# Layer 1's ring loads moved ahead of the couples' loads, and layer 4's gate and up products placed on either side of an older unit's down product

## The chip, the cores and the metric

The kernel runs on one core of one Trainium2 chip. The metric is the device time of one execution in microseconds (us).

## The reference, cut to what matters

Four conditional layers run one after the other on `x` (16 samples of 128 tokens by 128 features, float32), each added to its input. `cond_8` (16 x 8) chooses.

```python
# layer 1 (L0_cond in the reference): one expert of 8 for each sample
hidden = silu(x @ wu[e].T + bu) * (x @ wg[e].T + bg)   # 128 -> 256
x = x + hidden @ wd[e].T + bd                          # 256 -> 128
x = x + x @ W_base.T + b_base + lora(x, cond_8)        # layer 2
x = x + x @ w_bot(cond_8).T + bias                     # layer 3
# layer 4 (L3_cond): the two best of 8 experts for each sample, and a shared one
out = sum over the two e: w_e * (gelu(x @ gate_e) * (x @ up_e)) @ down_e    # 128 -> 512 -> 128
x = x + out + (gelu(x @ shared_gate) * (x @ shared_up)) @ shared_down
```

## The kernel before, in words

**Layer 1.** The 16 samples are taken in turn. Each needs its expert's pack (386.5 KB), which SyncE (SP) loads into `ring0`, a ring of 8 slots (`SLOTS0`); `load0(b)` (L255 to L260) does it. It reads sample b's expert number out of SBUF with a register load of its own (L256), waits from b = 8 on until sample b - 8 has been finished (`x1_done`), and issues the DMA (L259). TensorE runs `upgate0(b + 1)` ahead of `down0(b)` (L467, L475), ScalarE the SiLU (L392), VectorE the gate's multiply (L690) and the sum into `x` (L704).

**SP's order.** SP is one queue in program order: `load0` for samples 0 to 7, the shared expert's pack (768 KB), a wait for the sort of layer 4 (`slots_done`) and a register load of 24 expert numbers (L241), then `load_duo(0)` (L265), `load0(8)`, `load0(9)`, `load_duo(1)`, `load0(10)` to `load0(15)`, and the packs of the solos (L274). A couple's or a solo's pack has 768 KB. Later come the gathers of a couple's two samples (L282) and the remaining packs.

**Layer 4.** The work is cut into 48 units, in an order written out by hand in the list `ORDER`. An S unit is one quarter of the shared expert's hidden rows for 4 samples; a D unit is one half of a couple's hidden rows (a couple, `duo`, is two samples that use the same expert; 12 couples, two units each); an R unit is a solo, one sample with one expert. The order is SSSS DDSRDDSDDRS DDSRDDSDDRS DDSRDDSDDR DDRDDRDD SSSS. Units are numbered by their place; so 12 and 13 are a couple's second half and a solo, 18 and 19 a solo and a couple's first half. Nothing but the following is needed for each unit u:

- TensorE: the gate product G(u) into one PSUM bank, the up product U(u) into another, and later the down product D(u) into an accumulator. `gateup(u)` issues G(u) and U(u) (L520 for S, L530 for D, L537 for R); `down(u)` issues D(u) (L564 for S, L579 for D, L588 for R). The operands of S and D units are split into a high and a low part, three matmuls for each product.
- ScalarE: `gelu(u)` on the gate bank (L403), then `hid_hi`, the high part of the hidden rows (L422, not for R).
- VectorE: `product(u)`, gelu times up (L752); `hidden_low(u)`, the low part (L743, not for R); and for the last unit of a couple and for a solo `result(u)`: a register load of the batch numbers (L241) and one addition into `x_sum` for each sample (L769: two for a couple, one for a solo); for the last unit of a shared group one addition of 512 columns (L778).
- GpSimd (POOL): the split of each couple's pack in six pieces (L360 CAST, L363 TENSOR_TENSOR); it may begin on couple j when the last D of couple j - 2 is done.

VectorE's loop runs, at step u, `hidden_low(u - 1)`, `product(u)`, `result(u - 2)`, in this order. `product(u)` waits for `up_done`, which U(u) signals. D(u) of a couple's first half or a solo waits until `x_summed` counts the additions of the couple or solo before it, because all of these use the accumulator bank `acc[1]`. Where two such units are direct neighbours, the additions of the first have only the time between the two down products: pairs (couple's second half, solo) stand 5 times in the order, at units 12, 23, 34, 37 and 40 with the unit after each; pairs (solo, couple's first half) stand 6 times, at 7, 18, 29, 35, 38 and 41. Unit 43, a couple's second half, is followed by an S unit whose second half uses the same bank.

TensorE's loop of layer 4 (L599 to L602):

```python
for u in range(UNITS):
    if u + AHEAD < UNITS:      # AHEAD is 2
        gateup(u + AHEAD)
    down(u)
```

Of the kernel before, what the change touches and what calls it, by code (L numbers as in the profile page):

```python
# [22 lines left out]
P = 128  # L23
B = 16
E = 8
# [12 lines left out]
N2 = 2 * P  # L38
# [5 lines left out]
GATE3, UP3, DOWN3 = 0, H3, 2 * H3  # L44
# [17 lines left out]
SLOTS0 = 8  # L62
FREE = 2
PAIRS = 3
AHEAD = 2
SPLITS = 3
RAWS = 2
HALVES = 2
# [12 lines left out]
UNITS = len(ORDER)  # L81
# [33 lines left out]
def build_kernel(nc, xT, cond, condT, lora, small, w2, experts0, experts3, shared, out):  # L115
    ctx = ExitStack()
    with ctx:
# [3 lines left out]
        def sem(name):  # L121
            return ctx.enter_context(nc.semaphore(name))
# [33 lines left out]
        at_row = sb("at_row", [1, B], U32)  # L156
# [69 lines left out]
        gate_done, up_done, act_done, mul_done = sem("gate_done"), sem("up_done"), sem("act_done"), sem("mul_done")  # L226
# [13 lines left out]
        def values(engine, row, count=B):  # L240
            _, got = nc.values_load_multi_w_load_instructions(  # L241
                row, engines=(engine,), min_val=0, max_val=count - 1,
                skip_runtime_bounds_check_because="batch and expert numbers that the sort has put there itself")
            return got
# [4 lines left out]
        @block.sync  # L249
        def _(sp):  # L250
            sp.dma_start(cond_sb[:, :], cond).then_inc(cond_in, 16)
            sp.dma_start(lora_sb[:, :], lora).then_inc(lora_in, 16)
            sp.dma_start(w2_sb[:, :, :], w2).then_inc(w2_in, 16)

            def load0(b):  # L255
                at = sp.value_load(at_row[0:1, b:b + 1], min_val=0, max_val=E - 1)  # L256
                if b >= SLOTS0:
                    sp.wait_ge(x1_done, b - SLOTS0 + 1)
                sp.dma_start(ring0[:, b % SLOTS0, :], experts0[bass.ds(at, 1), :, :].rearrange("e p n -> p (e n)"))\  # L259
                  .then_inc(e0_in[b % SLOTS0], 16)  # L260

            def load_duo(j):
                if j >= RAWS:
                    sp.wait_ge(duo_lo_done, 3 * (j - RAWS + 1))
                sp.dma_start(raw_duo[:, j % RAWS, :],  # L265
                             experts3[bass.ds(duo_expert[2 * j], 1), :, :].rearrange("e p n -> p (e n)"))\
                  .then_inc(duo_in[j % RAWS], 16)

            def load_solo(r):
                if r == 0:  # L270
                    sp.wait_ge(shared_done, 1)
                if r >= RAWS:
                    sp.wait_ge(down_done, AT["R", r - RAWS, 0] + 1)
                sp.dma_start(raw_solo[:, r % RAWS, :],  # L274
                             experts3[bass.ds(solo_expert[r], 1), :, :].rearrange("e p n -> p (e n)"))\
                  .then_inc(solo_in[r % RAWS], 16)

            def gather_duo(j):
                if j >= GATHERS:
                    sp.wait_ge(up_done, AT["D", j - GATHERS, 1] + 1)  # L280
                for n in range(2):
                    sp.dma_start(x_duo[:, j % GATHERS, :, n * P:(n + 1) * P].bitcast(F32),  # L282
                                 x_hl[:, bass.ds(duo_batch[2 * j + n], 1), :, :].rearrange("p b h n -> p (b h) n")
                                 .bitcast(F32)).then_inc(x_duo_in[j % GATHERS], 16)

            sp.wait_ge(at_done, 1)
            for b in range(SLOTS0):
                load0(b)
            sp.dma_start(shared_sb, shared).then_inc(shared_in, 16)
            sp.wait_ge(slots_done, 1)  # L290
            duo_expert = values(mybir.EngineType.SP, slot_row[0:1, SLOTS:SLOTS + 2 * DUOS], E)
            load_duo(0)
            load0(SLOTS0)
            load0(SLOTS0 + 1)
            load_duo(1)
            for b in range(SLOTS0 + 2, B):
                load0(b)
            solo_expert = values(mybir.EngineType.SP, slot_row[0:1, SLOTS + 2 * DUOS:2 * SLOTS], E)
            load_solo(1)
            load_solo(0)  # L300
            duo_batch = values(mybir.EngineType.SP, slot_row[0:1, 0:2 * DUOS])
            load_duo(2)

            sp.wait_ge(x_lo_done, G)
            for j in range(GATHERS):
                gather_duo(j)
            for kind, n, part in ORDER:

                if kind == "R" and n + RAWS < SOLOS:
                    load_solo(n + RAWS)  # L310
                if kind == "D" and part == 1:
                    if n + 3 < DUOS:
                        load_duo(n + 3)
                    if n + GATHERS < DUOS:
                        gather_duo(n + GATHERS)

            sp.wait_ge(x_summed, SUMMED[ORDER[-1]] - 2)
            for g in range(G - 1):
                sp.dma_start(out[:, group(g)], x_sum[:, group(g)]).then_inc(stored, 16)
            for n in range(2):  # L320
                at = slice((G - 1) * N + n * N2, (G - 1) * N + (n + 1) * N2)
                sp.wait_ge(x_summed, SUMMED[ORDER[-1]] - 1 + n)
                sp.dma_start(out[:, at], x_sum[:, at]).then_inc(stored, 16)
            sp.wait_ge(stored, 16 * (G + 1))
# [101 lines left out]
        def _(pe):  # L426
# [25 lines left out]
            for k in range(E):  # L452
                n = G + k // 2
                if k % 2 == 0:
                    pe.wait_ge(prep_copied, n - 1)
                ins = pe.matmul(prep[n % 2][:, (k % 2) * B * R:(k % 2 + 1) * B * R], w2_sb[:, k, :],
                                y_delta[:, :, :].rearrange("p b j -> p (b j)"), start=True, stop=True)
# [25 lines left out]
            for k in range(K):  # L483
                ins = pe.matmul(prep[0][:, 0:3 * SLOTS].rearrange("p (v s) -> p v s", v=3), ones[:, :],
                                payload[:, :, k, :], start=(k == 0), stop=(k == K - 1))
# [10 lines left out]
            for g in range(G):  # L496
                pe.wait_ge(x1_done, GB * g + GB)
                for j in range(GB):
                    ins = pe.matmul(lin[g][:, j * P:(j + 1) * P], lin1[:, g * GB + j, :],  # L499
                                    x[:, cols(g * GB + j)], start=True, stop=True)  # L500
# [6 lines left out]
                                    x[:, cols(g * GB + j)], start=True, stop=True)  # L507
                ins.then_inc(lin_mm, 1)

            def gateup(u):  # L510
                kind, n, part = ORDER[u]
                gate, up = pair[u % PAIRS]
                if u >= PAIRS:
                    pe.wait_ge(mul_done, u - PAIRS + 1)
                if kind == "S":
                    pe.wait_ge(x_lo_done, n + 1)
                    for bank, base, done in ((gate, GATE3, gate_done), (up, UP3, up_done)):
                        at = slice(base + part * P, base + (part + 1) * P)
                        for m, (w, h) in enumerate(((shared_hi, 0), (shared_hi, 1), (shared_lo, 0))):
                            ins = pe.matmul(bank[:, :].rearrange("p (b n) -> p b n", n=P), w[:, at],  # L520
                                            x_hl[:, n * GB:(n + 1) * GB, h, :], start=(m == 0), stop=(m == 2))
                        ins.then_inc(done, 1)
                elif kind == "D":
                    pe.wait_ge(x_duo_in[n % GATHERS], 32 * (n // GATHERS + 1))
                    pe.wait_ge(duo_lo_done, 3 * n + 2)
                    for bank, base, done in ((gate, GATE3, gate_done), (up, UP3, up_done)):
                        for i in range(2):
                            at = slice(base + (2 * part + i) * P, base + (2 * part + i + 1) * P)
                            for m, (w, h) in enumerate(((duo_hi, 0), (duo_hi, 1), (duo_lo, 0))):
                                ins = pe.matmul(bank[:, i * N2:(i + 1) * N2], w[:, n % HALVES, at],  # L530
                                                x_duo[:, n % GATHERS, h, :], start=(m == 0), stop=(m == 2))
                        ins.then_inc(done, 1)
                else:
                    pe.wait_ge(solo_in[n % RAWS], 16 * (n // RAWS + 1))
                    for bank, base, done in ((gate, GATE3, gate_done), (up, UP3, up_done)):
                        for m in range(C3):
                            ins = pe.matmul(bank[:, m * P:(m + 1) * P],  # L537
                                            raw_solo[:, n % RAWS, base + m * P:base + (m + 1) * P],
                                            x[:, cols(solo_batch[n])], start=True, stop=True)
                        ins.then_inc(done, 1)  # L540
# [57 lines left out]
            pe.wait_ge(lin_read, 2 * G)  # L598
            for u in range(UNITS):  # L599
                if u + AHEAD < UNITS:  # L600
                    gateup(u + AHEAD)
                down(u)  # L602

        @block.vector
        def _(dve):
# [254 lines left out]
```

## Time and profile before

| | us |
|---|---|
| median of 3 runs (lowest, highest) | 158.79 (157.98, 159.51) |
| the profiled execution | 159.42 |
| its span, first to last instruction | 157.4 |
| TensorE busy in the span | 149.7 (95%) |
| VectorE busy | 113.0 (72%) |
| GpSimd busy | 93.5 (59%) |
| ScalarE busy | 71.5 (45%) |

The profiled execution lies 0.63 us above the median, and 2.02 us of it lie outside the span. In rows of a timeline the first number is the start in us from the span's start and the second the length; the engine follows (PE is TensorE, DVE VectorE, ACT ScalarE, POOL GpSimd, SPq the queue of SyncE), then the line of the code, the operation, output and inputs. What stands in brackets at the end is the idle time before it and what ended it. In the chain of work that ended last, a row is a piece: start, length, engine, tile, line and count of instructions.

### The profile page before, as it was taken

Reading aid. Unit: us, or ns where it says so; the run is one execution under the profiler, and the core shown is the slowest. Engines: PE = TensorE matmul, PEld = TensorE weight load, DVE = VectorE, ACT = ScalarE, POOL = GpSimd, SP = SyncE. Lnnn points to the kernel's source line nnn. Section 1 sums busy time; section 2 is a strip of 40 time slices with the busy share of each in tenths; the row PEclk is TensorE's granted clock in tenths of the full one; section 3 lists DMA queues with packets and bytes.
Section 4 is the critical chain, followed back from the end, with each engine's and each line's share of the span. In section 5 each row is a group of like instructions: output and inputs, shape, how many; then the busy total and the mean of one; then the engine's idle time right before and its main releaser. Section 6 shows DMA issues by size and latency. Waiting matters only on the chain.

```text
span 157.4 us, 3159 instructions
## 1 busy us (share of the span) xinstructions
PE 149.7 (95%) x1078; PEld 135.8 (86%) x1078; DVE 113.0 (72%) x229; ACT 71.5 (45%) x138; POOL 93.5 (59%) x95
## 2 busy tenths in 40 slices
PE   6999994899999999999999999999999999999992
PEld 2369994799998689999999989999989899999881
DVE  3785662466798767768786887696778977768772
ACT  2765441346055455444543635435454443346550
POOL 1002999999502400958995775998593989990000
PEclk9999999999999999999999999999999999999999
DMA  3999999996000568377076749158619119000051
GB/s 72 406 324 313 332 414 401 401 389 225 18 0 0 159 177 236 101 222 245 4 242 249 249 117 305 45 158 300 212 22 332 53 42 348 16 0 0 0 201 69
DMA packets 13336, 29.11 MB, mean 185 GB/s; under 512 B 1272, under 2 KB 7944, under 8 KB 13192
## 3 DMA queue, kind: packets, MB, share of 16 engines
q1 hardware_dynamic: 12896, 27.71, 51.9%
q10 hardware_dynamic: 424, 1.20, 1.9%
q8 instruction: 9, 0.15, 0.4%
q14 instruction: 7, 0.06, 0.1%
HBM read 24.71 MB, written 1.05 MB: 164 GB/s over the span
## 4 chain that ended last, share of the span: by engine, by line
PE 71%; SPq 8%; DMA 7%; DVE 7%; issue 3%; ACT 2%; ACTq 0%; DVEq 0%
PE pair L530 22%; PE acc L579 10%; PE pair L537 9%; PE pair L520 8%; DMA ring<-experts 6%; PE acc L564 5%; PE acc L588 5%; PE pair L467 4%; SPq L256 3%; SPq L259 3%; PE acc L429 2%; PE pair L499 2%; PE acc L475 2%; DVE hid L752 2%; ACT hid_hi L422 2%
## 5 line engine op out<-in xcount | busy, mean ns | idle before, releaser
L743 DVE TENSOR_TENSOR hid_lo<-hid,hid_hi 128x512 fp32r<-128x512 f32 (+1 forms) x41 | 40.1, 981 | 18.5 <-ACT hid_hi L422 17.9
L363 POOL TENSOR_TENSOR duo_lo<-raw_duo,duo_hi 128x512 fp32r<-128x512 f32 x36 | 46.3, 1286 | 2.9
L422 ACT ACTIVATE hid_hi<-hid 128x512 fp32r<-128x512 f32 (+1 forms) x41 | 25.4, 622 | 48.1 <-DVE hid L752 47.1
L360 POOL CAST duo_hi<-raw_duo 128x512 fp32r<-128x512 f32 x36 | 30.4, 845 | 22.1 <-PE acc L579 22.1
L530 PE MATMUL pair<-x_duo,duo_hi 128*128 128x256 f32 x192 | 35.9, 284 | 0.1
L752 DVE TENSOR_TENSOR hid<-pair,act 128x512 f32<-128x512 f32 (+1 forms) x49 | 32.8, 672 | 3.8 <-PE pair L530 2.8
L403 ACT ACTIVATE act<-pair 128x512 f32<-128x512 f32 x48 | 28.2, 587 | 7.3 <-PE pair L530 5.5
L530 PEld LDWEIGHTS pair<-x_duo,duo_hi 128*128 128x128 f32 x192 | 29.9, 189 | 1.0 <-DVE hid L752 0.3
L530 PE MATMUL pair<-x_duo,duo_lo 128*128 128x256 f32 x96 | 27.1, 283 | 0.0
L520 PE MATMUL pair<-x_hl,shared_hi 128*128 128x512 f32 x64 | 20.3, 399 | 0.0
L467 PE MATMUL pair<-x,ring 128*128 128x128 f32 x128 | 17.2, 277 | 2.8 <-DMA ring<-experts 2.8
L467 PEld LDWEIGHTS pair<-x,ring 128*128 128x128 f32 x128 | 15.6, 192 | 3.4 <-DMA ring<-experts 3.2
L690 DVE SCALAR_TENSOR_TENSOR hid<-pair,ring,act 128x128 f32<-128x128 f32 x32 | 9.8, 346 | 11.5 <-PE pair L467 11.5
L530 PEld LDWEIGHTS pair<-x_duo,duo_lo 128*128 128x128 f32 x96 | 18.1, 188 | 0.0
L392 ACT ACTIVATE act<-pair,ring 128x128 f32<-128x128 f32 x32 | 10.0, 363 | 14.4 <-PE pair L467 14.4
L537 PE MATMUL pair<-x,raw_solo 128*128 x128 | 15.6, 275 | 0.0
L537 PEld LDWEIGHTS pair<-x,raw_solo 128*128 128x128 f32 x128 | 15.2, 192 | 0.3
L579 PE MATMUL acc<-hid_hi,duo_hi 128*128 128x256 f32 x48 | 14.3, 298 | 0.0
L579 PE MATMUL acc<-hid_hi,duo_lo 128*128 128x256 f32 x48 | 13.5, 282 | 0.0
L579 PE MATMUL acc<-hid_lo,duo_hi 128*128 128x256 f32 x48 | 13.5, 282 | 0.0
L336 POOL TENSOR_TENSOR lin<-lora_raw,small_sb 128x512 f32<-128x512 f32 x4 | 5.0, 1273 | 13.9 <-DVE w_col L699 13.9
L520 PEld LDWEIGHTS pair<-x_hl,shared_hi 128*128 128x128 f32 x64 | 11.3, 188 | 1.9
(94 smaller groups left out, 209.0 us busy)
## 6 DMA issues: line engine op xcount, KB each, us to landing
raw_duo<-experts SPq DMA_DIRECT2D x12, 768.0 KB, 5.0
ring<-experts SPq DMA_DIRECT2D x16, 386.5 KB, 5.9
raw_solo<-experts SPq DMA_DIRECT2D x8, 768.0 KB, 5.0
x_duo<-x_hl SPq DMA_DIRECT2D x24, 128.0 KB, 3.6
x<-xT ACTq DMA_DIRECT2D x1, 1024.0 KB, 6.0
raw_solo<-shared SPq DMA_DIRECT2D x1, 768.0 KB, 6.9
out<-lora_raw SPq DMA_DIRECT2D x3, 256.0 KB, 2.8
w_sb<-w SPq DMA_DIRECT2D x1, 512.0 KB, 4.0
```

The lines of the kernel that those rows point to most:

```text
L360: pool.tensor_copy(duo_hi[:, j % HALVES, piece(n)], raw_duo[:, j % RAWS, piece(n)])\
L363: pool.tensor_tensor(duo_lo[:, j % HALVES, piece(n)], raw_duo[:, j % RAWS, piece(n)], duo_hi[:, j % HALVES, piece(n)].bitcast(F32), ALU.su ...
L392: act.activation(act0[:, b % FREE, c, :], pair[b % FREE][0][:, c * P:(c + 1) * P], ACT.Silu, bias=ring0[:, b % SLOTS0, BUP0 + c:BUP0 + c + ...
L403: act.activation(act3[:, u % PAIRS, :], pair[u % PAIRS][0][:, :], ACT.Gelu_apprx_tanh)\
L422: act.activation(hid_hi[:, k % SPLITS, at], hid3[:, u % PAIRS, at], ACT.Copy)\
L467: ins = pe.matmul(pair[b % FREE][half][:, c * P:(c + 1) * P], ring0[:, b % SLOTS0, base + c * P:base + (c + 1) * P], x[:, cols(b)], start= ...
L520: ins = pe.matmul(bank[:, :].rearrange("p (b n) -> p b n", n=P), w[:, at], x_hl[:, n * GB:(n + 1) * GB, h, :], start=(m == 0), stop=(m == 2))
L530: ins = pe.matmul(bank[:, i * N2:(i + 1) * N2], w[:, n % HALVES, at], x_duo[:, n % GATHERS, h, :], start=(m == 0), stop=(m == 2))
L537: ins = pe.matmul(bank[:, m * P:(m + 1) * P], raw_solo[:, n % RAWS, base + m * P:base + (m + 1) * P], x[:, cols(solo_batch[n])], start=Tru ...
L579: ins = pe.matmul(y, w[:, n % HALVES, at], v[:, k, i * N2:(i + 1) * N2], start=(part == 0 and i == 0 and m == 0), stop=(part == 1 and i == ...
L743: dve.tensor_tensor(hid_lo[:, k % SPLITS, at], hid3[:, u % PAIRS, at], hid_hi[:, k % SPLITS, at].bitcast(F32), ALU.subtract).then_inc(hid_ ...
L752: dve.tensor_tensor(hid3[:, u % PAIRS, at], pair[u % PAIRS][1][:, at], act3[:, u % PAIRS, at], ALU.mult).then_inc(mul_done, 1)
```

## The change

Two edits. In SP's program the expert numbers of layer 1 are read with two loads of several registers (samples 0 to 3, then 4 to 15) and no longer one by one; and `load0(8)` to `load0(11)` stand ahead of the wait for `slots_done`, the register load of 24 numbers and `load_duo(0)`; `load0(12)` and `load0(13)` stand between the couples' first two loads, `load0(14)` and `load0(15)` behind them. In TensorE's loop the unit's gate product is issued first, then the older unit's down product, then the unit's up product. Nothing else is changed; the loops of VectorE and ScalarE are the same.

```diff
             def load0(b):
-                at = sp.value_load(at_row[0:1, b:b + 1], min_val=0, max_val=E - 1)
+                at = expert0[b]
                 if b >= SLOTS0:
                     sp.wait_ge(x1_done, b - SLOTS0 + 1)
...
             sp.wait_ge(at_done, 1)
-            for b in range(SLOTS0):
+            expert0 = list(values(mybir.EngineType.SP, at_row[0:1, 0:4], E))
+            for b in range(4):
+                load0(b)
+            expert0 += values(mybir.EngineType.SP, at_row[0:1, 4:B], E)
+            for b in range(4, SLOTS0):
                 load0(b)
             sp.dma_start(shared_sb, shared).then_inc(shared_in, 16)
+            for b in range(SLOTS0, SLOTS0 + 4):
+                load0(b)
             sp.wait_ge(slots_done, 1)
             duo_expert = values(mybir.EngineType.SP, slot_row[0:1, SLOTS:SLOTS + 2 * DUOS], E)
             load_duo(0)
-            load0(SLOTS0)
-            load0(SLOTS0 + 1)
+            for b in range(SLOTS0 + 4, SLOTS0 + 6):
+                load0(b)
             load_duo(1)
-            for b in range(SLOTS0 + 2, B):
+            for b in range(SLOTS0 + 6, B):
                 load0(b)
...
-            def gateup(u):
+            def gateup(u, which=(0, 1)):
...
-                    for bank, base, done in ((gate, GATE3, gate_done), (up, UP3, up_done)):
+                    for bank, base, done in (((gate, GATE3, gate_done), (up, UP3, up_done))[i] for i in which):
...
             for u in range(UNITS):
                 if u + AHEAD < UNITS:
-                    gateup(u + AHEAD)
+                    gateup(u + AHEAD, (0,))
                 down(u)
+                if u + AHEAD < UNITS:
+                    gateup(u + AHEAD, (1,))
```

## Rows read from the trace of the kernel before

**Rows 1.** The page's second part, the span in 40 equal slices.

```profile
PEclk9999999999999999999999999999999999999999
GB/s 72 406 324 313 332 414 401 401 389 225 18 0 0 159 177 236 101 222 245 4 242 249 249 117 305 45 158 300 212 22 332 53 42 348 16 0 0 0 201 69
```

**Rows 2.** The chain that ended last, in order of time, layer 1's last stall.

```profile
20.97 8.77 DMA ring<-experts
29.78 1.16 PE pair L467 x8
...
31.39 0.89 PE pair L467 x8
```

**Rows 3.** Timeline of TensorE, layer 1: sample 7's, 8's and 10's first products.

```profile
22.50 1.06 PE L467 MATMUL pair<-x,ring 128*128 128x128 f32 x8
...
26.06 1.16 PE L467 MATMUL pair<-x,ring 128*128 128x128 f32 x8 [2.06 <-DMA ring<-experts]
...
29.78 1.16 PE L467 MATMUL pair<-x,ring 128*128 128x128 f32 x8 [0.78 <-DMA ring<-experts]
```

**Rows 4.** Timeline of SyncE's queue and of VectorE, samples 8 to 10 and sample 0's end.

```profile
17.80 1.45 SPq L259 DMA_DIRECT2D ring<-experts  x2
...
16.10 0.34 DVE L704 SCALAR_TENSOR_TENSOR x<-acc,ring,x 128x128 f32<-128x128 f32 x1
```

**Rows 5.** Register loads (shortest, median, longest ns), and the page's sixth part.

```profile
L241 SPq TENSOR_LOAD <-slot_row x3: 534/1431/1452, 15.1 to 30.7; - x3
...
ring<-experts SPq DMA_DIRECT2D x16, 386.5 KB, 5.9
```

**Rows 6.** The chain in layer 4: down(12), gateup(15), down(13), gateup(16), down(14), gateup(17), down(15), gateup(18).

```profile
77.33 0.71 PE acc L579 x6
78.04 1.43 PE pair L530 x12
79.48 0.89 PE acc L588 x8
80.37 1.44 PE pair L530 x12
81.80 0.69 PE acc L564 x3
82.50 1.39 PE pair L520 x6
83.89 0.71 PE acc L579 x6
84.60 1.78 PE pair L537 x16
```

**Rows 7.** Timeline of VectorE: product(14), result(12), hidden_low(14), product(15), result(13), hidden_low(15).

```profile
77.44 0.69 DVE L752 TENSOR_TENSOR hid<-pair,act 128x512 f32<-128x512 f32 x1 [0.46 <-PE pair L520]
78.23 0.61 DVE L769 SCALAR_TENSOR_TENSOR lora_raw<-acc,w_col,lora_raw 128x128 f32 x2
78.89 1.81 DVE L743 TENSOR_TENSOR hid_lo<-hid,hid_hi 128x512 fp32r<-128x512 f32 x1
80.63 0.68 DVE L752 TENSOR_TENSOR hid<-pair,act 128x512 f32<-128x512 f32 x1
81.23 0.34 DVE L769 SCALAR_TENSOR_TENSOR lora_raw<-acc,w_col,lora_raw 128x128 f32 x1
82.06 1.04 DVE L743 TENSOR_TENSOR hid_lo<-hid,hid_hi 128x512 fp32r<-128x512 f32 x1 [0.50 <-ACT hid_hi L422]
```

**Rows 8.** Timeline, the end: VectorE's product(47) and hidden_low(47), TensorE's down(47).

```profile
151.99 0.76 DVE L752 TENSOR_TENSOR hid<-pair,act 128x256 f32<-128x256 f32 x2
...
153.44 0.38 PE L564 MATMUL acc<-hid_hi,shared_hi 128*128 128x256 f32 x1
```

**Rows 9.** Timeline, layer 4's beginning: hidden_low(1) on VectorE, down(1) on TensorE.

```profile
51.48 1.03 DVE L743 TENSOR_TENSOR hid_lo<-hid,hid_hi 128x512 fp32r<-128x512 f32 x1 [0.70 <-ACT hid_hi L422]
...
52.56 0.50 PE L564 MATMUL acc<-hid_hi,shared_hi 128*128 128x512 f32 x1 [0.39 <-DMA x_duo<-x_hl]
```

**Rows 10.** Timeline of GpSimd beside hidden_low(14).

```profile
78.18 0.61 POOL L360 CAST duo_hi<-raw_duo 128x512 fp32r<-128x512 f32 x1
78.88 1.28 POOL L363 TENSOR_TENSOR duo_lo<-raw_duo,duo_hi 128x512 fp32r<-128x512 f32 x1
```

More of the change, by code:

```diff
@@ L525, in gateup @@
                     pe.wait_ge(duo_lo_done, 3 * n + 2)
-                    for bank, base, done in ((gate, GATE3, gate_done), (up, UP3, up_done)):
-                        for i in range(2):
-                            at = slice(base + (2 * part + i) * P, base + (2 * part + i + 1) * P)
+                    for bank, base, done in (((gate, GATE3, gate_done), (up, UP3, up_done))[i] for i in which):
+                        for half in range(2):
+                            at = slice(base + (2 * part + half) * P, base + (2 * part + half + 1) * P)
                             for m, (w, h) in enumerate(((duo_hi, 0), (duo_hi, 1), (duo_lo, 0))):
-                                ins = pe.matmul(bank[:, i * N2:(i + 1) * N2], w[:, n % HALVES, at],
+                                ins = pe.matmul(bank[:, half * N2:(half + 1) * N2], w[:, n % HALVES, at],
                                                 x_duo[:, n % GATHERS, h, :], start=(m == 0), stop=(m == 2))
@@ L534, in gateup @@
                     pe.wait_ge(solo_in[n % RAWS], 16 * (n // RAWS + 1))
-                    for bank, base, done in ((gate, GATE3, gate_done), (up, UP3, up_done)):
+                    for bank, base, done in (((gate, GATE3, gate_done), (up, UP3, up_done))[i] for i in which):
                         for m in range(C3):
```

## The prediction

> **What bounds the kernel now.** I read the page's slices first. The granted clock is full in all 40, so TensorE runs at the upper of its two levels (2.4 GHz) to the end, and what has to be found is idle time and not slow time; the GB/s line shows a load phase of 313 to 414 GB/s that ends in slice 10 and a thin traffic after it [rows 1]. The chain of waits came next. Up to 38 us it has SP's queue and one wait for a ring slot's DMA, 8.77 us from issue to use, and then TensorE in layer 1 [rows 2]. From 52 to 145 us it is TensorE piece on piece, down product and gate-up product in turn, without a wait of note [rows 6]. So layer 1 waits for its ring, and layer 4 is bound by TensorE in program order. What there counts for the change is how near the other engines run behind it; for that I read VectorE's timeline [rows 7].
>
> **Part 1, layer 1.** TensorE takes 0.89 us for a sample's four up and gate products and 0.45 for its down product [rows 2], 1.34 a sample. Sample 7 starts at 22.50, so 8 could start at 23.84; it starts at 26.06. From there 10 could start at 28.74 or, with the 0.1 us by which a first product after a wait is longer, at 28.84; it starts at 29.78 [rows 3]. The stalls take 2.22 + 0.94 = 3.16 us.
>
> In the new order `load0(8)` waits only for sample 0 (16.44, [rows 4]) in place of the 17.80 at which it is issued now, behind the register load of 1.45 us and a couple's 768 KB. Samples 1 to 3 come free every 1.34 us, so 9, 10 and 11 are issued at about 17.8, 19.1 and 20.6. With the ring's median of 5.9 us to landing [rows 5] they land at 22.3, 23.7, 25.0 and 26.5 and are needed at 23.8, 25.2, 26.5 and 27.9: in time. The price is on the couples' side: everything behind `load0(11)` moves to after 20.6, plus 1.45 us for the 24 numbers. `load_duo(0)` is issued at about 22.7 and not 16.7, then 12, 13, couple 1, 14, and 15 when sample 7 is done (about 25.8). These are 2 x 768 + 4 x 386.5 = 3,082 KB, 3.16 MB; at 400 GB/s [rows 1] they take 7.9 us, and with 1.5 to 2 us before the first bytes the last lands at about 32.2. Sample 14 is needed at 31.9 and 15 at 33.2, so each has between half a microsecond and a microsecond to spare. I count 3.0 of the 3.16; bounds 3.16 and nothing, or a loss of 1 us if the burst lands that much later than counted (the slowest ring load took 8.77 us [rows 2]). GpSimd takes up couple 0 at 30.1 in the trace, after the shared pack's split, and couple 1 at 35.8; both have landed by then. Reading the numbers in two loads takes the single register loads out of the first eight issues; the first may come later by the difference of two loads (a load of several took at least 0.53 us [rows 5]). Either is hidden, since samples 1 to 7 run at TensorE's own pace already; uncovered, it would be those 0.5 us once.
>
> **Part 2, layer 4's order.** No matmul is added. What changes is when the others hear of them. Write G, U, D for the three products. Before: G(u+2) U(u+2) D(u) G(u+3) U(u+3) D(u+1). After: G(u+2) D(u) U(u+2) G(u+3) D(u+1). Half of 1.44 is 0.72 for a D unit's gate or up product, half of 1.39 is 0.70 for S, half of 1.78 is 0.89 for R; the down products take 0.71, 0.69 and 0.89 [rows 6]. Between D(u) and D(u+1) still stand two products. But VectorE's program has `product(u+2)` ahead of `result(u)`, and `product(u+2)` needs U(u+2), which now comes behind D(u). So the additions for unit u can't begin when D(u) ends; they begin an up product and a multiply later.
>
> *Couple, then solo (5 pairs; worked at 12 and 13).* Now U(14) ends with the chain's piece at 77.33, `product(14)` starts at 77.44, the first addition at 78.23, and both are done at 78.84; D(13) comes at 79.48 [rows 6, 7]. They have 0.64 us to spare. In the new order, counted from U(14)'s end: 0.11 to the product, 0.79 to the additions, 0.61 for both, 0.05 to TensorE (a DVE end at 52.51 and its waiter at 52.56 [rows 9]) are 1.56; D(13) is due after G(15), at 0.72. Wait 0.84. A first group after a wait is longer: 1.16 for 0.89 [rows 2], so 0.27 more. 1.11 each, 5.55 in all.
>
> *Solo, then couple (6 pairs; 4 with a D or S gate product between, 2 with a solo's).* One addition, 0.60 after the product's start and 0.34 long [rows 7]: 0.11 + 0.60 + 0.34 + 0.05 = 1.10, due at 0.70: wait 0.40, with the refill 0.67, four times 2.7. Behind a solo's gate product, 0.89: 0.21 + 0.27 = 0.48, twice 1.0. Together 3.7.
>
> *Couple 11, then the S unit 44.* Only its second half uses the bank: due at 0.70 + 0.35 = 1.05, ready at 1.56: 0.51 + 0.27 = 0.8.
>
> *The end.* D(47) waits now for VectorE and ScalarE: product at 151.99, and 153.44 for the down product [rows 8]. That chain starts at U(47). Before, D(45) and D(46) stand behind it; now only D(46), for D(45) goes first. U(47) ends 0.70 later, so does the kernel: +0.7.
>
> *The beginning.* D(1) waits for `hid_lo` at 52.51, in either order [rows 9]; the profile names a DMA there, but the low part ends 0.05 us before. Now U(3) is done by then; in the new order it comes behind: +0.7, bounds 0 and 0.7.
>
> Sum of layer 4: 5.55 + 3.7 + 0.8 + 0.7 + 0.7 = 11.4 us. Lower bound 8.1: no refill beyond 0.1, and couple's additions at 0.64 after the product as at unit 18. Upper bound: what follows. D(u) also waits for `hid_lo(u)`. From U(u)'s end this takes 0.11 + 1.45 to its start, 1.04 as at unit 15, 0.06: 2.66 [rows 7]. The new order gives it 0.72 + 0.71 + 0.72 + 0.72 = 2.87 where the old one gave 4.3. That is enough by 0.2 us, no more. But unit 14's took 1.81, and it started within 0.01 us of a GpSimd subtraction of 1.28 us [rows 10]: 3.43, or 0.56 too long. Five units have 1.77 to 1.82, all right after a solo; 5 x (0.56 + 0.27) = 4.1. I take none of it, because the pair stalls sit in the same places and cover most, and GpSimd's phase will be another. Upper bound 15.5.
>
> The Trainium skill (SBUF — State Buffer, section "SBUF: two separate sides") says that a VectorE operation with two SBUF inputs and a GpSimd operation that reads SBUF exclude each other, whoever starts first holding the shared ports for the whole instruction. Rows 7 and 10 agree: the subtraction ends at 80.16 and `hid_lo` 0.54 us later. By this rule the whole 4.1 us could come on top (159.4 - 3.0 + 15.5 = 171.9); by the rows' usual 1.04 nothing does.
>
> **Sum.** 159.42 - 3.0 + 11.4 = 167.8 for an execution like the profiled one, its span 165.8. The profiled one lies 0.63 above the median of the runs shown, so against that 158.79 + 8.4 = 167.2.
>
> **The rivals.**
> *A. VectorE's order doesn't bind.* If the additions still come in time at all 12 places, because VectorE runs late already and U's delay is swallowed there, 10.05 us fall away: 158.79 - 3.0 + 1.4 = 157.2, faster. For it: VectorE lags up to 1.2 us behind TensorE (product(15) starts at 80.63, U(15) ended before 79.48), and then 0.7 later costs it nothing. Against: the due time comes 0.72 earlier too, and the spare time at the pairs is 0.64 (12) and less. It decides at 0.7 us of spare time. 10%.
> *B. The ring gains nothing.* Couples and samples 12 to 15 now wait in one burst, and samples 14 and 15 are late by what 8 and 10 lose now. 158.79 + 11.4 = 170.2. For it: no more than a microsecond to spare. 8%.
> *C. `hid_lo` becomes the bound.* 2.66 of 2.87 us, and over it wherever GpSimd is in the way: 158.79 - 3.0 + 15.5 = 171.3. 10%.
> *D. Layer 4's order has no effect either way, the stalls being hidden by gelu starting earlier:* it starts when the gate is done, but `product` needs U as well. It would be A without its 1.4: 155.8. 1%.
>
> **How the numbers follow.** The forecast has the rest, 71%, with its own bounds 158.79 - 3.16 + 8.1 = 163.7 and about 170. The range goes from 162.5 to 171: below to half of the small losses being absent as well, above into B and C. A and D are left out. This kernel's runs tell about 1% from no change (1.6 us). A ends just at that mark: faster 0.07, same 0.06, slower 0.87.
>
> **What would show it.** In layer 1: samples every 1.34 us, no wait for the ring, layer 4 beginning 3 us earlier (TensorE's first L520 at 42.8 where it is at 45.8). In layer 4: VectorE's additions L769 (couples) and L769 (solos) named as what D waits for, 11 waits of 0.4 to 1.1 us, `product` (L752) waiting for TensorE at most units where now it waits 5 times, and TensorE's busy share near 90%. At the end about 1.0 us idle before the last down product where now there is 0.3. Wrong: if no L769 ends a wait of TensorE, A is the case; if L743 ends most, C; if the ring's DMA still does, B.

## The result, and the profile after

172.61 us is the median of 6 runs after (171.03 to 173.77), 158.91 that of 6 runs before (157.98 to 159.56): 1.086 times as long, 95% interval 1.080 to 1.092. In this document medians are over all runs, while ratios and their intervals leave out a kernel's slowest runs (over 1.5% above its fastest), which takes out five of ten in e1, three of six in e8 and four of twelve in e11. I had forecast slower, 167.2, and at most 171. Slower it is, by 13.7 us and not 8.4.

The chain after at the pair of units 12 and 13, the place worked out in the prediction:

```profile
79.27 0.71 PE pair L526 x3
...
80.07 0.56 DVE hid L760
...
80.93 0.19 issue
81.12 0.35 DVE lora_raw L777
81.47 0.14 issue
81.61 1.13 PE acc L594 x8
82.74 0.74 PE pair L536 x6
```

U(14) ends at 79.98, `product(14)` starts at 80.07, the couple's second addition ends at 81.47, and the solo's down product begins at 81.61. Before, the same product stood in an unbroken row of TensorE pieces [rows 6]. The list of waits after says what TensorE waited for:

```profile
PE acc L594 <- DVE lora_raw L777: 5.0, 5, 1.3
...
PEld acc L585 <- DVE hid_lo L751: 3.7, 4, 1.0
PEld acc L570 <- DVE hid_lo L751: 2.9, 4, 1.0
PE acc L585 <- DVE lora_raw L777: 2.8, 6, 0.6
...
PE acc L570 <- DVE lora_raw L777: 0.5, 1, 0.5
```

Columns: who waits, for what; us in total, times, longest. L594, L585 and L570 are the down products (L588, L579, L564 before), L777 the addition, L751 `hid_lo`. The 5 + 6 + 1 waits for the addition are the twelve neighbours counted in the prediction, all there and no other.

Layer 4, from its first product to its last, can be read off both timelines: 45.76 to 154.41 before, 46.38 to 168.25 after, 108.65 against 121.87 us. That is 13.2 of the 13.8 by which the profiled executions differ (span 157.4 and 171.2). I set the steps from each product's start to the next one's against the same steps in an undisturbed stretch. A row holds the wait before the down product and the extra length of that product after a wait (0.07 to 0.11), as the forecast's terms do:

| place | times | forecast | after |
|---|---|---|---|
| couple, then solo | 5 | 5.55 | 1.16 + 1.15 + 1.15 + 1.54 + 1.17 = 6.2 |
| solo, then couple | 6 | 3.7 | 0.74 + 0.82 + 0.82 + 0.63 + 0.63 + 0.75 = 4.4 |
| couple 11, then S | 1 | 0.8 | 0.8 |
| `hid_lo` late, units 15 and 26 | 2 | none | 0.70 + 0.73 = 1.4 |
| end | 1 | 0.7 | 0.7 |
| beginning | 1 | 0.7 | 0.5 |
| small late places of before that are gone | 4 | none | -0.7 |
| sum | | 11.4 | 13.3 |

The sum meets the 13.2 to 0.1 us.

Layer 1 did not follow. TensorE's timeline after, samples 12 to 14:

```profile
31.42 1.16 PE L473 MATMUL pair<-x,ring 128*128 128x128 f32 x8
...
32.86 1.10 PE L473 MATMUL pair<-x,ring 128*128 128x128 f32 x8
...
35.77 1.16 PE L473 MATMUL pair<-x,ring 128*128 128x128 f32 x8 [1.36 <-DMA ring<-experts]
```

The stalls at samples 8 and 10 [rows 3] are gone, and sample 14 is 1.57 us late, sample 12 by 0.14. From the first sample's products to the last one's layer 1 takes 37.21 - 14.84 = 22.37 in place of 36.58 - 12.76 = 23.82 us: 1.45 gained. But the first sample starts at 14.84 and not at 12.76. What stands ahead of it, the loras' products, before and after (shortest, median, longest ns):

```profile
L446 PE MATMUL pair<-bs_w,lora_sb x8: 592/592/697, 5.4 to 8.6; 128*128 128x512 f32 x8
```

```profile
L452 PEld LDWEIGHTS pair<-bs_w,lora_sb x8: 186/310/337, 5.5 to 10.3; 128*128 128x128 f32 x8
L452 PE MATMUL pair<-bs_w,lora_sb x8: 592/1021/1222, 5.5 to 10.7; 128*128 128x512 f32 x8
```

The same matmuls take 1.7 times as long in the median (1,021 ns against 592), and the longest 1,222. The lower of TensorE's two levels (1.2 GHz) would fit that, but the profile gives the granted clock as 1.00 in that stretch too, so this cause is not shown. Whether the change does that had to be asked.

### The profile page after: what moved, and what is told of

It is laid out like the page before. It is cut to its first block, busy times and chain, and to the rows that moved or that the text cites. A ratio compares the mean times of both kernels' runs of the same rounds, so it can differ in the third digit from the quotient of the medians.

```text
span 171.2 us, 3158 instructions
## 1 busy us (share of the span) xinstructions
PE 155.1 (91%) x1078; PEld 136.9 (80%) x1078; DVE 108.9 (64%) x229; ACT 71.1 (41%) x138; POOL 93.6 (55%) x95
## 4 chain that ended last, share of the span: by engine, by line
PE 64%; DVE 18%; issue 5%; DMA 5%; ACT 4%; SPq 1%; DVEq 1%; ACTq 0%
PE pair L536 14%; PE acc L585 11%; PE pair L543 7%; DVE hid L760 7%; PE pair L526 6%; DVE hid_lo L751 5%; PE pair L473 5%; PE acc L570 5%; DMA ring<-experts 5%; ACT hid_hi L428 4%; PE pair L452 3%; PE acc L594 3%; DVE lora_raw L777 3%; PE acc L481 2%; PE pair L462 2%
## 5 line engine op out<-in xcount | busy, mean ns | idle before, releaser
L369 POOL TENSOR_TENSOR duo_lo<-raw_duo,duo_hi 128x512 fp32r<-128x512 f32 x36 | 47.6, 1322 | 2.9
L760 DVE TENSOR_TENSOR hid<-pair,act 128x512 f32<-128x512 f32 (+1 forms) x49 | 33.1, 677 | 21.0 <-PE pair L536 12.9
L751 DVE TENSOR_TENSOR hid_lo<-hid,hid_hi 128x512 fp32r<-128x512 f32 (+1 forms) x41 | 34.0, 831 | 18.8 <-ACT hid_hi L428 18.2
L366 POOL CAST duo_hi<-raw_duo 128x512 fp32r<-128x512 f32 x36 | 29.2, 810 | 28.7 <-PE acc L585 28.7
L536 PE MATMUL pair<-x_duo,duo_hi 128*128 128x256 f32 x192 | 37.2, 288 | 0.0
L536 PEld LDWEIGHTS pair<-x_duo,duo_hi 128*128 128x128 f32 x192 | 30.7, 189 | 1.5
L585 PE MATMUL acc<-hid_hi,duo_hi 128*128 128x256 f32 x48 | 14.7, 306 | 3.7 <-DVE lora_raw L777 2.8
L543 PE MATMUL pair<-x,raw_solo 128*128 x128 | 16.9, 275 | 0.0
L543 PEld LDWEIGHTS pair<-x,raw_solo 128*128 128x128 f32 x128 | 15.9, 192 | 0.3
L398 ACT ACTIVATE act<-pair,ring 128x128 f32<-128x128 f32 x32 | 10.0, 364 | 12.9 <-PE pair L473 12.9
L585 PEld LDWEIGHTS acc<-hid_hi,duo_hi 128*128 128x128 f32 x48 | 9.1, 189 | 6.7 <-DVE hid_lo L751 3.7
L585 PE MATMUL acc<-hid_hi,duo_lo 128*128 128x256 f32 x48 | 13.5, 282 | 0.0
L585 PE MATMUL acc<-hid_lo,duo_hi 128*128 128x256 f32 x48 | 13.5, 282 | 0.0
## 6 DMA issues: line engine op xcount, KB each, us to landing
ring<-experts SPq DMA_DIRECT2D x16, 386.5 KB, 6.0
```

The lines of the kernel that those rows point to most:

```text
L366: pool.tensor_copy(duo_hi[:, j % HALVES, piece(n)], raw_duo[:, j % RAWS, piece(n)])\
L369: pool.tensor_tensor(duo_lo[:, j % HALVES, piece(n)], raw_duo[:, j % RAWS, piece(n)], duo_hi[:, j % HALVES, piece(n)].bitcast(F32), ALU.su ...
L398: act.activation(act0[:, b % FREE, c, :], pair[b % FREE][0][:, c * P:(c + 1) * P], ACT.Silu, bias=ring0[:, b % SLOTS0, BUP0 + c:BUP0 + c + ...
L536: ins = pe.matmul(bank[:, half * N2:(half + 1) * N2], w[:, n % HALVES, at], x_duo[:, n % GATHERS, h, :], start=(m == 0), stop=(m == 2))
L543: ins = pe.matmul(bank[:, m * P:(m + 1) * P], raw_solo[:, n % RAWS, base + m * P:base + (m + 1) * P], x[:, cols(solo_batch[n])], start=Tru ...
L585: ins = pe.matmul(y, w[:, n % HALVES, at], v[:, k, i * N2:(i + 1) * N2], start=(part == 0 and i == 0 and m == 0), stop=(part == 1 and i == ...
```

## The experiments

Theory 1: layer 4's order costs all of it, by additions that stand on VectorE behind a product that needs the later up product; the ring gained some 1.5 us. Rivals: the ring's edit is itself a loss by way of the late start; VectorE's pace, or GpSimd beside `hid_lo`, is the bound.

**e1 and e2: each edit alone.** e1 is the kernel after with layer 4's loop of before, e2 the kernel before with layer 4's loop of after:

```diff
                 if u + AHEAD < UNITS:
-                    gateup(u + AHEAD, (0,))
+                    gateup(u + AHEAD)
                 down(u)
-                if u + AHEAD < UNITS:
-                    gateup(u + AHEAD, (1,))
```

> The SP edits alone; layer 4 in the order of before. Theory 1 (the whole loss is layer 4's order, the ring gained about 1.5 us): 1.5 us below the kernel before, about 157.4. Rival (the ring's edit is itself a loss, because the profiled execution after starts layer 1 2.1 us later): 0.5 us or more above it, about 159.5. As I had forecast it: 3.0 below, 155.9.

> Layer 4's new order alone; SP's program of before. Theory 1: 13.2 us above the kernel before, about 172. Rival: the two edits work against each other, and the order alone costs the 11.4 us forecast or less, 170.3 at most.

Measured: e2 172.25 us against 159.44, ratio 1.084 (1.075 to 1.093); layer 4 takes 168.21 - 46.40 = 121.81, the time of after to 0.1 us. The order is the loss; that the two edits work on each other doesn't show. e1: 160.19 against 159.44, ratio 1.004 (0.996 to 1.011): nothing that can be told, and not the 157.4 of theory 1, though its profiled execution (157.85) is 1.57 faster than that of before. Its times lie apart, 157.85 to 158.70 (4 runs) and 160.01 to 161.18 (6). And e2, with SP's program of before, starts its first sample at 14.97. So the late start isn't the ring's.

**e11 and e12: the ring again, and the kernel before again.**

> The kernel of e1_ring_only again, for its spread. Theory (the ring gains 1.7 us only in executions whose first sample starts at 12.8, and nothing at 14.8): two groups of times, near 158 and near 160.5, the median within 1 us of the kernel before. Rival (a plain loss): all above it.

> The kernel before, for a second profile. Theory (the start at 12.8 or 14.8 is a matter of the execution and of no edit): either start can come; with the late one the stalls at samples 8 and 10 shrink to about 1.7 us, and layer 4 starts at 46.4, as in e2_order_only, which has the same SP program.

e12, the kernel before, has the late start as well:

```profile
L446 PE MATMUL pair<-bs_w,lora_sb x8: 592/1061/1222, 5.5 to 11.0; 128*128 128x512 f32 x8
```

Its profile beside those of before, e1 and e11:

| kernel | SP's program | first sample | last sample | layer 4 starts | span |
|---|---|---|---|---|---|
| before | before | 12.76 | 36.58 | 45.76 | 157.4 |
| e12 | before | 15.17 | 36.68 | 45.85 | 157.4 |
| e1 | after | 12.76 | 34.84 | 44.02 | 155.8 |
| e11 | after | 14.74 | 37.45 | 46.63 | 158.4 |

Before, a start 2.4 us later costs little: the waits for the ring shrink from 3.2 to 1.0 us, less than the 1.7 expected, and layer 4 starts 0.1 us later. In e2, which has the same program of SP and starts at 14.97, they shrink to 1.7, and layer 4 starts at 46.40, 0.6 later. So one kernel's profiles differ by half a microsecond here, and the four rows of the table alone prove little. The other profiles with SP's program of after (e3 to e7) bear out the direction: in the five with the early start, e1 among them, layer 4 begins at 43.65 to 45.08, 0.7 to 2.1 us ahead of before's 45.76; in the three with the late one (after, e6, e11) at 46.22 to 46.63, between 0.2 ahead of e2 and 0.8 behind e12.

e11's median is 160.30 against 159.20, ratio 1.003 (0.998 to 1.009). The mean of all 22 times of e1 and e11 is 159.85, that of the 36 of the kernel before beside them 158.98. The ring's edit gains nothing on the whole and may lose a little, and its direction goes with a start that no edit here touches. SP's timelines fit that. In e11 couple 0's load is issued at 24.78 and the last ring load lands at 36.95; in e1, with the early start, at 22.80 and 34.32. In e12 against the profile of before the couple's issue moves by as much (18.74 and 16.70), but the last ring load lands at 34.83 and 34.68. So in SP's program of after a late start delays the last packs, and in that of before it doesn't.

**e3: the additions first.** The kernel after, with VectorE's order turned:

```diff
+                result(u - 2)
                 if u < UNITS:
                     product(u)
-                result(u - 2)
```

> The kernel after, with VectorE's result(u - 2) issued ahead of product(u). Theory 1 (TensorE waits at the 12 neighbours because the additions stand behind a product that needs the later up product; 11.3 us of waits counted in the profile after): these go, 172.6 - 11.3 = 161.3, and TensorE no longer waits for L777's successor. Rival (VectorE as a whole is too slow for the new order, hid_lo first): the waits only change their name, 168 or more.

Measured 164.86 (163.63 to 167.06), ratio 1.031 (1.020 to 1.042) to before; layer 4 takes 159.77 - 44.71 = 115.1, 6.8 less than after. No solo's down product is late; after a solo two are, by 0.2. So the order of VectorE's program is what made the pairs wait. But 4.5 us less was gained than the pairs' 11.3, and the median lies 3.6 above the 161.3 expected, for something new is late at units 11, 22 and 33, by 1.3 each. TensorE, VectorE and GpSimd at unit 11:

```profile
73.27 1.27 POOL L369 TENSOR_TENSOR duo_lo<-raw_duo,duo_hi 128x512 fp32r<-128x512 f32 x1
73.37 1.71 DVE L751 TENSOR_TENSOR hid_lo<-hid,hid_hi 128x512 fp32r<-128x512 f32 x1 [0.76 <-ACT hid_hi L428]
...
75.14 0.39 PE L585 MATMUL acc<-hid_hi,duo_hi 128*128 128x256 f32 x1 [1.02 <-DVE hid_lo L751]
```

`hid_lo` starts 0.10 us after GpSimd's subtraction and ends 0.54 after it. That is rival C, at units where `hid_lo` was never late in the kernel after.

**e6 and e7: GpSimd out of the way.** Both cut GpSimd's split of couples 2 to 11 to 8 columns of 512 a piece, so most of these weights' split is left out; e6 on top of e3, e7 on the kernel after:

```diff
-                    pool.tensor_copy(duo_hi[:, j % HALVES, piece(n)], raw_duo[:, j % RAWS, piece(n)])\
+                    at = piece(n) if j < HALVES else slice(n * H3, n * H3 + 8)
+                    pool.tensor_copy(duo_hi[:, j % HALVES, at], raw_duo[:, j % RAWS, at])\
```

> e3_sum_first with GpSimd's split of couples 2 to 11 cut to 8 of 512 columns a piece, which leaves out most of the split of these couples' weights. Theory (the three waits of 1.2 to 1.3 us left in e3 come from hid_lo beside GpSimd's subtraction): they go, and 164.9 falls by 3.8 or more, to 161 or below. Rival (hid_lo is late by VectorE's own order): 164 or more.

> The kernel after with the same cut of GpSimd's split. Theory 1 (pair waits have nothing to do with GpSimd): the 11.3 us of pair waits stay, the two hid_lo waits of 0.7 at units 15 and 26 go: 172.6 - 1.4 = 171.2, some tenths less if the solo-couple pairs were lengthened by a late hid_lo. Rival C (hid_lo and GpSimd are the bound): 166 or less.

e6: 162.05 (4 runs, 159.46 to 162.39), 2.8 below e3 where 3.8 was expected; its profiled execution has the late start, e3's the early one, and layer 4 alone takes 156.78 - 46.22 = 110.6, 4.5 below e3's. The three waits are gone. e7: 169.89 against the 171.2 expected, ratio 1.073 (1.062 to 1.085); layer 4 takes 163.91 - 43.65 = 120.3, 1.6 below after's. Its waits:

```profile
PE acc L595 <- DVE lora_raw L778: 5.0, 5, 1.3
...
PE acc L586 <- DVE lora_raw L778: 2.7, 6, 0.5
...
PE acc L571 <- DVE lora_raw L778: 0.5, 1, 0.5
```

These are the twelve pair waits of after to 0.1 us, with GpSimd nearly idle. The longest `hid_lo` takes 1.031 us there, and 1.691 after. So GpSimd's part is the 1.4 us at units 15 and 26 and some 0.2 more at units 19 and 30, and the pair waits don't need it.

The Trainium skill (SBUF — State Buffer, section "SBUF: two separate sides") says that such a VectorE operation and a GpSimd operation that reads SBUF exclude each other for the whole instruction. The trace of e3 agrees with 1.71 against the 0.69 us of an undisturbed one. What it doesn't give is how often they meet: after, `hid_lo` takes 1.57 to 1.69 us three times (units 15, 26 and 37), of which TensorE waits for two; in e3 1.71 to 1.72 three times, and it waits for all.

**e4 and e5: the old order at the ends.** e4 goes back to both products ahead where the older unit is a couple's second half or a solo, e5 at both units of each of the 12 pairs (there `late` is `not {u, u - 1} & {7, 12, 18, 23, 29, 34, 35, 37, 38, 40, 41, 43}`):

```diff
+                late = ORDER[u] not in END_AT
                 if u + AHEAD < UNITS:
-                    gateup(u + AHEAD, (0,))
+                    gateup(u + AHEAD, (0,) if late else (0, 1))
                 down(u)
-                if u + AHEAD < UNITS:
+                if late and u + AHEAD < UNITS:
```

> The kernel after, but where the older unit is a couple's second half or a solo (20 of 48) both products of the unit ahead are issued in front of its down product, as before; the other 28 keep the new order. Theory 1: the 12 pair waits (11.3 us) go, some hid_lo waits, the beginning and the end (2 us) stay: about 160 to 161.5. Rival (the new order costs by itself at every unit): 28 of 46 of the 13.2 us stay, 157.4 + 8.0 = 165.4.

> The kernel after, with both products of the unit ahead issued in front of the down product again at the two units of each of the 12 pairs (20 or so units), so that the pair has two products between its down products and VectorE has the later up product before them. Theory 1: all pair waits go (11.3 us of the 172.6), hid_lo, beginning and end stay: 161 to 162. Rival (spacing isn't it; VectorE's pace is): 166 or more.

Measured: e4 163.18, ratio 1.027 (1.019 to 1.036), above the 160 to 161.5 of theory 1. The mixed order does something that neither order does: after a solo in the old order and a couple's first half in the new, only one product stands between the two down products. Unit 8 in its timeline:

```profile
67.34 0.34 DVE L778 SCALAR_TENSOR_TENSOR lora_raw<-acc,w_col,lora_raw 128x128 f32 x1
...
67.83 0.36 PE L585 MATMUL acc<-hid_hi,duo_hi 128*128 128x256 f32 x1 [0.42 <-DVE lora_raw L778]
```

Four more such places (19, 30, 36, 39) lose 0.5 to 0.7 us and one 0.2; with unit 8 that is 3.3 us, which covers the excess. e5 keeps two products between: 159.94, ratio 1.007 (1.003 to 1.012); layer 4 takes 155.06 - 45.08 = 110.0. Not one pair is late, nor `hid_lo`; what is left over before's 108.65 is the beginning and the end. That is below the 161 to 162 expected, because no `hid_lo` is late. The new order at the remaining units gains nothing either; it costs the 1.3 us by which layer 4 is longer.

**e8, e9, e10: what the ring can gain.** e8 is the kernel before with the numbers read in two loads and nothing else. e9 has `load0(8)` and `load0(9)` ahead of the wait for the sort, 10 and 11 between the couples' loads and the rest behind; e10 has all eight ahead:

```diff
             sp.dma_start(shared_sb, shared).then_inc(shared_in, 16)
+            for b in range(SLOTS0, B):
+                load0(b)
             sp.wait_ge(slots_done, 1)
...
             load_duo(0)
-            load0(SLOTS0)
-            load0(SLOTS0 + 1)
             load_duo(1)
-            for b in range(SLOTS0 + 2, B):
-                load0(b)
```

> The kernel before, with the expert numbers read by two loads of several registers; order of the loads and of layer 4 as before. If SP's pace of issue (1.1 us for each 386.5 KB) is what keeps the transfers at 310 to 340 GB/s between 8 and 20 us, the first eight land earlier, the stall of 3.2 us at samples 8 and 10 shrinks by 1 to 2 us: 157.5 to 158.5 against 159.4. If the ring's order behind the couple's pack is the whole cause: no change.

> e8 and load0(8), load0(9) ahead of the wait for the sort, load0(10) and load0(11) between the couples' loads, the rest behind; layer 4 as before. If the ring of after loses its gain because four loads, each waiting for a sample, keep the transfers at 295 GB/s from 20 to 28 us, two such loads leave less of a gap: samples without a wait for the ring, 3 us of stall gone in executions that start early, 156.5 to 157.5 against 159.4. Rival: the gain is lost to the start anyway, within 0.5 us of e1's 160.2.

> Numbers read as in after, all of load0(8) to load0(15) ahead of the sort's wait and of the couples' packs; layer 4 as before. Theory (the ring's late samples are those behind a couple's pack; GpSimd has 8 us to spare for the couples): no wait for the ring at all, GpSimd's split 1 to 2 us later and still in time; layer 4 starts at about 42.7 us where the first sample starts at 12.8, and at 44.6 where it starts at 14.8; median 1.8 to 3 us below the kernel before. Rival (what the couples lose comes back): GpSimd or TensorE waits for a couple's pack, no gain.

e8: medians 159.28 and 159.28, ratio 0.990 (0.982 to 0.997). The interval says faster by one per cent, but it rests on three of six runs; the medians say nothing. Its profile has the late start and waits 1.4 us for the ring, between e12's 1.0 and e2's 1.7. I call it open. e9: 159.95 against 159.28, 1.003 (0.999 to 1.008), with a late start and samples late at three places (0.7, 0.35, 1.6): no gain, as the rival had it. e10: 158.51 against 159.20, 0.999 (0.994 to 1.004). Its ring is what part 1 of the prediction wanted: no sample late, the last one at 33.30, layer 4 at 43.26. The 2.5 us don't arrive. GpSimd waits for the couples' packs, and its split now lies beside VectorE's low parts of `x`:

```profile
34.88 0.61 POOL L362 CAST duo_hi<-raw_duo 128x512 fp32r<-128x512 f32 x1 [4.58 <-DMA raw_duo<-experts]
...
43.66 1.30 POOL L365 TENSOR_TENSOR duo_lo<-raw_duo,duo_hi 128x512 fp32r<-128x512 f32 x1
```

```profile
43.70 1.81 DVE L719 TENSOR_TENSOR x_hl<-x,x_hl 128x512 fp32r<-128x512 f32 x1
```

Such a low part takes 0.68 us before, when GpSimd is through at 41.6. Three of the four low parts are longer (1.48, 1.81, 1.21), and layer 4 takes 153.49 - 43.26 = 110.2, 1.6 more than before, all of it ahead of its third down product. I had looked at when TensorE needs the couples (53 us) and found 8 us to spare; the spare time was VectorE's. No version here is shown to beat the kernel before.

## Why the prediction was right or wrong

**Direction and cause: right.** That `product(u+2)` stands ahead of `result(u)` and now needs an up product behind D(u) is the loss: 12 waits at the 12 places, gone when VectorE's order is turned (e3) or the spacing comes back (e5). Rivals A and D fall with e2. B came true beside it (e1).

**Couple, then solo: right in kind, 5.55 against 6.2.** The chain has 1.49 from U(14)'s end to the last addition's (0.09 + 0.78 + 0.62), and 0.14 from there to TensorE in place of the 0.05 that I took from `hid_lo`: a wait of 0.91 and not 0.84. Unit 38's 1.54 has 0.4 us of its own: `product(40)` starts at 143.73, 0.42 us after VectorE could have issued it, for nothing that the profile shows; this stays open.

**Solo, then couple: 3.7 against 4.4.** At unit 19 `product(20)` starts at 95.56 and the addition at 96.16, 0.60 later as in the rows; but that product starts behind a `hid_lo` of 1.04, 0.20 after U(20)'s end and not 0.11, and again 0.14 stand where I had 0.05.

**`hid_lo` at nothing: wrong by 1.4.** I held that the pair stalls would cover it. Right after solos, where the rows had the long ones, none is left; at units 15 and 26, the second unit after a solo, it is late, and with GpSimd out of the way it isn't (e7).

**Part 1 is the step that failed, 3.0 against nothing on the whole.** After, layer 4 starts at 46.38 where 42.8 was forecast, 3.6 late (the 3.0 not gained, and 0.6 lost with the late start), and takes 1.8 longer: together the 5.4 us by which the span of 171.2 misses the 165.8. In e1, which has the early start of the rows, the times of issue came as worked out, couple 0 at 22.8. What failed is "at 400 GB/s they take 7.9 us", to 32.2. From e1, SP's timeline first and then the chain:

```profile
22.80 0.33 SPq L265 DMA_DIRECT2D raw_duo<-experts  x1
```

```profile
25.02 8.34 DMA ring<-experts
...
33.40 1.16 PE pair L473 x8
```

Sample 14's pack lands at 33.36 and is needed at 32.18; the last one lands at 34.32, 2.1 us later than counted. The windows of e1:

```profile
20.00:24.00 4.00, 4.00 (x38) 4.00 (x38) 2.74 (x10) 1.87 (x6) 4.00 (x7) 1.00 0.93 301
24.00:28.00 4.00, 4.00 (x38) 4.00 (x38) 2.58 (x10) 1.88 (x6) 3.92 (x4) 1.00 0.83 289
28.00:32.00 4.00, 3.96 (x36) 3.77 (x35) 2.28 (x9) 1.77 (x6) 3.92 (x3) 1.00 1.00 394
```

The last two columns are the share of the transfer engines and GB/s. For 8 us they move 289 to 301, where before has 416 and 398 between 20 and 28. Four ring loads, each waiting for a sample, ask for no more: 386.5 KB every 1.34 us are 295 GB/s. Then nothing is issued from 21.14 to 22.80, and between 24 and 25 us only 111 GB/s move. So at 28 us there is a backlog, and sample 14 pays. The low rate alone isn't the fault: e10 has 288 and 313 in the same windows and no sample late, for there no couple's pack stands ahead of a sample's. I saw the burst's thin margin and gave its failure 8%. And the sum stood on one profiled execution, which had the early start; with the late one only 1.0 (e12) to 1.7 us (e2) of the 3.16 are there to be gained.

**The signs.** All 12 pair waits name the additions, TensorE's busy share is 91%, and `product` waits for TensorE 22 times where it waited 5 times: fewer than "most units", yet the mechanism. Of layer 1's signs none came but the stalls at samples 8 and 10, which went. The lower bound of layer 4, 8.1, doesn't come out of its two conditions, which make 7.7 or, with the beginning, 8.4; nothing hangs on it.

**The range.** Its upper end, 171, took in a lost ring (170.2) or a part of a late `hid_lo`, not a lost ring together with a sum of layer 4 that is 1.8 us too small; both came.

## What to carry to other kernels

When an order is changed on one engine, write the program order of the engines that feed it beside the new one, and look for a step that waits for the later signal and stands ahead of the step that is needed sooner. Count how much room two uses of one accumulator have in the old order (0.64 us here) before taking any of it away. And where a stall on a load is to go, ask in a second profile whether it is there in every execution, and what the later loads will then lie beside.

## What the runs showed of the hardware that I had not expected

The same program begins in two ways. In 7 of 14 profiled executions the loras' products take 592 or 593 ns (median) and the first sample starts at 12.6 to 12.9 us; in the other 7 they take 852 to 1,061 ns, and it starts at 14.6 to 15.2. The kernel before is on both sides, and so is the ring's edit; the granted clock is given as full in both. What decides it stays open. From the end of a VectorE addition to the matmul that waited for it 0.14 us pass (81.47 to 81.61 at unit 13), from the end of `hid_lo` 0.06 (86.67 to 86.73 at unit 15, 75.08 to 75.14 in e3).
